# Centring the first half ahead of layer 1 and scaling by the reciprocal deviation after the expert pick

## The reference, cut to what matters

```python
def _layernorm(x, axis=-1, eps=1e-05):
    m = jnp.mean(x, axis=axis, keepdims=True)
    v = jnp.var(x, axis=axis, keepdims=True)
    return (x - m) / jnp.sqrt(v + eps)

# layer 1, E = 4 experts, W = ctx_2048, expert_ids from the token id
for e in range(E):
    g = jax.nn.silu(jnp.einsum('bsd,fd->bsf', hidden_states, Wg[e]))
    u = jnp.einsum('bsd,fd->bsf', hidden_states, Wu[e])
    y = jnp.einsum('bsf,df->bsd', g * u, Wd[e])
    out = jnp.where((expert_ids == e)[..., None], y, out)
x = x + layer_1(_layernorm(x))
x = x + layer_2(_layernorm(x))
```

## Time and profile before

| | us |
|---|---|
| median of 3 runs | 173.74 |
| lowest, highest of them | 173.63, 174.43 |
| the profiled execution, whole | 173.89 |
| its span in the trace | 171.8 |
| TensorE busy in the span | 166.6 (97%) |
| VectorE busy | 114.2 (66%) |
| ScalarE busy | 67.8 (39%) |
| GpSimd busy | 39.6 (23%) |

### The profile page before, as it was taken

The page is one execution under the profiler, slowest core; times in us unless marked ns, Lnnn a source line. Parts: engine busy times, 40 slices in busy tenths (PEclk is TensorE's granted clock), DMA queues, the critical chain, the costliest instruction groups (busy, mean ns, idle before and its releaser), DMA issues.

```text
span 171.8 us, 2194 instructions
## 1 busy us (share of the span) xinstructions
PE 166.6 (97%) x728; PEld 130.6 (76%) x728; DVE 114.2 (66%) x230; ACT 67.8 (39%) x112; POOL 39.6 (23%) x37
## 2 busy tenths in 40 slices
PE   6989999999999999999999999999999999999992
PEld 2568888888877888788787778788787887878881
DVE  0779778888984988588688528964744444444452
ACT  2472520551258254824664593152212222223320
POOL 2593000698200025539385000000000000000000
PEclk9999999999999999999999999999999999999999
DMA  4999000176400036742111200043361211100003
GB/s 137 307 373 352 23 4 2 25 236 227 122 0 4 15 130 181 203 160 67 61 61 61 61 0 4 8 126 126 113 195 45 75 65 61 62 0 4 2 0 122
DMA packets 7971, 16.41 MB, mean 95 GB/s; under 512 B 1336, under 2 KB 2200, under 8 KB 7832
## 3 DMA queue, kind: packets, MB, share of 16 engines
q1 hardware_dynamic: 7960, 16.27, 29.0%
HBM read 15.08 MB, written 1.18 MB: 95 GB/s over the span
## 4 chain that ended last, share of the span: by engine, by line
PE 97%; ACT 0%; POOL 0%; DVE 0%; issue 0%; DVEq 0%; POOLq 0%
PE bank L853 26%; PE bank L913 14%; PE bank L911 13%; PE bank L912 13%; PE bank L931 7%; PE bank L934 7%; PE bank L932 7%; PE bank L943 4%; PE bank L820 2%; PE bank L907 1%; PE bank L908 1%; PE bank L832 1%; ACT xn_hi L433 0%; POOL warm L383 0%; DVE xt L732 0%
## 5 line engine op out<-in xcount | busy, mean ns | idle before, releaser
L913 PE MATMUL bank<-xn_lo,gu_hi 128*128 128x512 f32 (+1 forms) x104 | 41.0, 394 | 0.0
L911 PE MATMUL bank<-xn_hi,gu_lo 128*128 128x512 f32 x96 | 37.9, 395 | 0.0
L912 PE MATMUL bank<-xn_hi,gu_hi 128*128 128x512 f32 x96 | 37.8, 394 | 0.0
L501 ACT ACTIVATE h_hi<-hid 128x512 fp32r<-128x512 f32 (+1 forms) x26 | 16.4, 632 | 45.7 <-DVE hid L720 45.7
L725 DVE TENSOR_TENSOR h_lo<-hid,h_hi 128x512 fp32r<-128x512 f32 (+1 forms) x26 | 20.2, 778 | 15.6 <-ACT h_hi L501 15.6
L913 PEld LDWEIGHTS bank<-xn_lo,gu_hi 128*128 128x128 f32 (+1 forms) x104 | 19.4, 186 | 5.0
L491 ACT ACTIVATE act_sb<-bank 128x512 f32<-128x512 f32 (+1 forms) x26 | 15.4, 594 | 18.1 <-PE bank L913 18.0
L398 POOL TENSOR_TENSOR gu_lo<-stage,gu_hi 128x512 fp32r<-128x512 f32 x12 | 17.9, 1516 | 17.6 <-ACT gu_hi L426 17.6
L912 PEld LDWEIGHTS bank<-xn_hi,gu_hi 128*128 128x128 f32 x96 | 18.0, 187 | 4.4
L911 PEld LDWEIGHTS bank<-xn_hi,gu_lo 128*128 128x128 f32 x96 | 18.0, 187 | 4.4
L931 PE MATMUL bank<-h_hi,wd_lo 128*128 128x512 f32 (+1 forms) x52 | 20.6, 396 | 0.0
(11 more groups left out here) (76 smaller groups left out, 213.1 us busy)
## 6 DMA issues: line engine op xcount, KB each, us to landing
stage<-gu_d SPq DMA_DIRECT2D x6, 512.0 KB, 3.5
stage<-wd_d SPq DMA_DIRECT2D x3, 512.0 KB, 4.1
x<-comb_d SPq DMA_DIRECT2D x8, 192.0 KB, 2.7
ids<-comb_d SPq DMA_DIRECT2D x8, 192.0 KB, 3.0
stage<-ctx_d SPq DMA_DIRECT2D x4, 256.0 KB, 5.0
xt<-xt_d SPq DMA_DIRECT2D x1, 1024.0 KB, 10.3
x<-comb_d SPq DMA_DIRECT2D x8, 128.0 KB, 3.1
ids<-comb_d SPq DMA_DIRECT2D x8, 128.0 KB, 2.8
```

Of the source, the lines that this page charges most:

```text
L911: nc.tensor.matmul(out[:], gu_lo[:, cols], xn_hi[:, h, k], start=(k == 0), stop=False)
L912: nc.tensor.matmul(out[:], gu_hi[:, cols], xn_hi[:, h, k], start=False, stop=False)
L913: ins = nc.tensor.matmul(out[0:rows, :], gu_hi[:, wide], xn_lo[:, h, k], start=False, stop=(k == KC - 1))
```

## The change

x of half 0 is only centred before layer 1: TensorE multiplies (x - mean), and the reciprocal deviation of each token multiplies the picked product z of mixes 0 and 1 (`scale`). As that product has tokens on columns, the deviations are needed as a row on all partitions: they are written to DRAM from their tile with four bytes per piece, and read back broadcast to 128 partitions. Half 1 and layer 2 are normalised as before. The mean of VectorE's tiles (0 and 2) comes from its statistics, that of ScalarE's tiles (1 and 3) from an accumulating pass (`minus_mean`). The identity comes in one load with the first two tiles. The first half of `xn_hi` is rounded by ScalarE for k = 0 and by VectorE for k = 1. Mix 0 has an order of its own (`first_mix`), in which the matmuls with the low weights of experts 1 to 3 come later. The warm-up has 8 matmuls, with 8 shorter ones placed between and behind the transposes. The diff, cut to its core:

```diff
-WARM_UP = 20
+WARM_UP = 8
...
             sp.dma_start(ids[:], ids_d.partition_broadcast(P)).then_inc(ids_in, 16)
+            sp.wait_ge(powered, 1)
+            sp.dma_start(rstd_d.rearrange("t c -> c t"), rstd[:, 0], allow_slow_non_contiguous=True).then_inc(rstd_out, 16)
+            sp.wait_ge(rstd_out, 16)
+            sp.dma_start(rstd_all[:], rstd_d.rearrange("t c -> (t c)").partition_broadcast(P)).then_inc(rstd_in, 16)
+            sp.wait_ge(rstd_in, 16)
             sp.dma_start(xt[:], xt_d).then_inc(xt_in, 16)
...
             nc.gpsimd.memset(comb[:], 0.0).then_inc(comb_zero, 1)
-            rstd_of(0, 1, slice(0, TT // 2))
-            rstd_of(0, 2, slice(TT // 2, TT))
-            for n in range(E1):
-                low_part(n)
-            rstd_of(1, 3)
+            low_part(0)
+            low_part(1)
+            rstd_of(0)
+            low_part(2)
+            low_part(3)
+            rstd_of(1)
...
+            def centre(t):
+
+                act.wait_ge(x_in[t // (TT // 2)], 16)
+                nc.scalar.activation(xn[:, t], x[:, t], ACT.Copy, scale=-1.0 / D,
+                                     accum_out=minus_mean[:, t:t + 1]).then_inc(astep, 1)
+                act.wait_ge(astep, t // 2 + 1)
+                nc.scalar.activation(xn[:, t], x[:, t], ACT.Identity, bias=minus_mean[:, t:t + 1]).then_inc(normed_a, 1)
...
             nc.scalar.preload_act_table(ACT.Silu)
-            apply_norm(0, range(TT // 2))
+            centre(1)
+            centre(3)
             high_part(0)
-            apply_norm(0, range(TT // 2, TT))
+            x_high("n1", 0, 0)
             high_part(1)
-            x_high("n1", 0, 0)
-            x_high("n1", 0, 1)
             high_part(2)
             high_part(3)
             first_z(0)
             apply_norm(1)
-            silu_z(0)
             first_z(1)
             x_high("n1", 1, 0)
             x_high("n1", 1, 1)
+            silu_z(0)
             silu_z(1)
...
+            def centre(t):
+
+                dve.wait_ge(x_in[t // (TT // 2)], 16)
+                tile_stats(0, t)
+                dve.wait_ge(dstep, steps[0])
+                step(nc.vector.bn_aggr(meanvar[:, 0, t], stats[:, t]))
+                dve.wait_ge(dstep, steps[0])
+                nc.vector.tensor_scalar(xn[:, t], x[:, t], meanvar[:, 0, t, 0:1], None, ALU.subtract).then_inc(normed_v, 1)
+
+            def scale(n):
+
+                dve.wait_ge(rstd_in, 16)
+                dve.wait_ge(z_picked, (n + 1) * (E1 - 1))
+                nc.vector.tensor_tensor(prod[:, n % 2], prod[:, n % 2], rstd_all[:], ALU.mult).then_inc(z_scaled, 1)
...
+            centre(0)
+            centre(2)
+            tile_stats(0, 1)
+            dve.wait_ge(side_done, side_at["n1", 0, 1] + 1)
+            nc.vector.tensor_scalar(xn_hi[:, 0, 1], side_bank("n1", 0, 1)[:], 1.0, None, ALU.mult).then_inc(xhi_done, 1)
             x_low("n1", 0, 0)
             x_low("n1", 0, 1)
+            tile_stats(0, 3)
+            layer_norm_vars(0, (1, 3))
...
             pick(0, masked[0], [1])
             layer_norm_apply(1)
             pick(0, masked[0], [2, 3])
-            hidden_1(0)
+            scale(0)
             x_low("n1", 1, 0)
             x_low("n1", 1, 1)
+            hidden_1(0)
             pick(1, masked[0])
+            scale(1)
             hidden_1(1)
...
+                pe.wait_ge(xhi_done, KC)
+                high(0)
+                weights_low(0, last=False)
+                high(1)
+                x_low(0, last=True)
+                x_low(1)
+                weights_low(1)
+                high(2)
+                x_low(2)
+                high(3)
+                x_low(3)
+                weights_low(2)
+                weights_low(3)
...
             pe.wait_ge(warm_set, 1)
-            for _ in range(WARM_UP):
-                nc.tensor.matmul(bank[7][:], warm[:, 0:P], warm[:], start=True, stop=True)
-            pe.wait_ge(consts_in, 16)
-            norm_transposes("n1", 0, 0)
-            mix(0)
+            keep_warm(WARM_UP)
+            pe.wait_ge(x_in[0], 16)
+            norm_transposes("n1", 0, 0, (0, 2, 2, 1))
+            keep_warm(3, HALF // 2)
+            first_mix()
```

More of the change, by code:

```diff
@@ L60 @@
 SPREADS = 4
+PAIR = TT // 2 * D
 RING = HALVES * KC
@@ L453, in silu_z @@
             def silu_z(n):
-                act.wait_ge(z_picked, (n + 1) * (E1 - 1))
+                if mixes[n][1] == 0:
+                    act.wait_ge(z_scaled, n + 1)
+                else:
+                    act.wait_ge(z_picked, (n + 1) * (E1 - 1))
                 if n >= 2:
@@ L812, in side_wait, with keep_warm, norm_transposes @@
                 return bank[b]
-            def norm_transposes(what, n, h):
+            def keep_warm(count, cols=HALF):
+                for _ in range(count):
+                    nc.tensor.matmul(bank[7][:, 0:cols], warm[:, 0:P], warm[:, 0:cols], start=True, stop=True)
+            def norm_transposes(what, n, h, between=()):
                 banks = [side_wait(what, h, k) for k in range(KC)]
                 for t in range(TT):
+                    if between:
+                        keep_warm(between[t], HALF // 2)
                     wait_normed(pe, n, t)
@@ L875, in mix, with first_mix, high, weights_low @@
                         between[e]()
+            def first_mix():
+                z = [ring_bank("z", 0, e)[:] for e in range(E1)]
+                f = slice(0, P)
+                def high(e):
+                    pe.wait_ge(w_hi, e + 1)
+                    for k in range(KC):
+                        nc.tensor.matmul(z[e], ctx_hi[:, e, k, f], xn_hi[:, 0, k], start=(k == 0), stop=False)
+                def weights_low(e, last=True):
+                    pe.wait_ge(w_lo, e + 1)
+                    for k in range(KC):
+                        ins = nc.tensor.matmul(z[e], ctx_lo[:, e, k, f], xn_hi[:, 0, k], start=False, stop=last and k == KC - 1)
+                    if last:
+                        ins.then_inc(z_done, 1)
+                def x_low(e, last=False):
+                    for k in range(KC):
+                        pe.wait_ge(xlo_done, k + 1)
+                        ins = nc.tensor.matmul(z[e], ctx_hi[:, e, k, f], xn_lo[:, 0, k], start=False, stop=last and k == KC - 1)
+                    if last:
+                        ins.then_inc(z_done, 1)
+                pe.wait_ge(xhi_done, KC)
[11 more added lines that the diff above has]
+                weights_low(3)
             def gate_or_up(g, up):
```

82 lines of the change are left out of this document (36 added, 46 removed).

## The result

The change is slower by far more than forecast: 186.84 us median (186.68 to 188.38, four runs) for 173.88 of the kernel before on the same chip (173.63 to 174.43, four runs), a ratio of 1.076, 95% interval 1.0697 to 1.0823. The prediction was 174.7 with a range up to 176.6. The direction was right, the size was not. The profiled execution has a span of 184.5 us for 171.8, so 12.7 us are to be found.

The account below looks back on a forecast made before the run. TensorE, busy 97% of the span, was taken as the bound, with VectorE having 1.28 us to spare. Opening -0.6 and stall +1.5 gave +0.95 on the profiled execution: 174.7 us predicted, range 173.3 to 176.6 (forecast's own 174.1 to 175.4).

Parts of the forecast that it names:

- The place and the chain of VectorE: First `x_low` of half 1 to `pick(4)` grows from 16.75 to 19.35 us; TensorE stalls 1.52 us for x1.
- The row by DMA: Deviations through DRAM: write 3.6 us, broadcast 2.9, row there at 18.5 (16.9 to 21.7), just in time for `scale(0)`.
- Rival A: The row comes late, each us past 18.7 a us of stall: total +2.2 to +4, about 176; chance 0.22.
- Size of the last add: Last add before x1's transposes takes 0.69 us if ahead of GpSimd's subtraction, up to 1.76 if behind: stall 1.1 to 2.2.
- Rival B: TensorE's clock is not up when mix 0 begins, transposes take 1 us more: about +1.7, 175.4; chance 0.10.
- The opening: Centring only, before layer 1: first matmul near 8.65, mix 1 at 15.0 instead of 15.58; gain 0.6 us, bounds 0 and 1.3.
- M: Time at which mix 1 can begin: 15.58 us in the kernel before, forecast 15.0.
- So no second stall follows: Behind the x1 stall both engines are delayed alike; VectorE waits 0.71 us for ScalarE before layer 2's critical `x_low`.

Follow-up runs that it names:

- row_at_once_full: Changed kernel without the row's two DMAs (half 0 deviations set to 1), shared down weights' low part on 128 partitions instead of 96: 175.69 us, ratio 1.0097.
- row_by_pe: Changed kernel with the row made by TensorE transposes and a ScalarE copy, shared down weights' low part on 128 partitions: 175.82 us, ratio 1.0116.
- price_writes: Kernel before plus six DMAs in a row behind its last output: 512 adjoining 4-byte pieces 8.23 us, spaced 256 B apart 2.13, 128 of 16 B 1.41.
- wd0_full: Changed kernel with the shared down weights' narrow piece cut on all 128 partitions instead of 96: 181.29 us, ratio 1.0432.
- fill_waits: Changed kernel with matmuls on zeros in TensorE's two long waits (20 and 22): 184.82 us.
- row_at_once_order: As row_at_once_full, with `hidden_1(0)` put back ahead of the two `x_low` of half 1: 175.73 us.
- opening: Kernel before with merged load, 14 warm-ups and fillers, split rounding and `first_mix`; half 0 normalised as before, no row or scaling: 179.94 us, ratio 1.0360.
- opening_full: As opening, with the shared down weights' low part cut on all 128 partitions: 174.53 us, ratio 1.0039.
- relief: row_by_pe with half 1's masks made by GpSimd and the first step of `pick(2)` moved into the wait for silu: 173.66 us, ratio 0.9997.
- gap: Changed kernel with GpSimd waiting, after its 96-partition subtraction, until VectorE has done `add_block_1(3)`: 180.08 us, ratio 1.0346.

## Why the prediction was wrong, point by point

**The place and the chain of VectorE: right.** The second stall stands where the prediction put it, released by `add_block_1`, and 19.35 us from `x_low` to `pick(4)` were measured as 19.34 (row_at_once_full) and 19.32 (row_by_pe). The stall came out as 1.70 to 1.73 in the trace's count, or 2.16 for 1.52 in the forecast's own (row_at_once_full), inside 1.1 to 2.2 either way.

**"The row by DMA": the first step that failed, by a mis-sized term.** The prediction had 3.6 for the write and 2.9 for the broadcast, bounds 5.8 and 3.9; they took 8.82 and 4.96. Its argument was that the time lies between "does not hang on pieces" and "hangs on pieces alone", both read from a store of 128 long pieces. Neither end covers it: spaced pieces, equal in number, took 2.13 us (price_writes). Pow ended at 10.74 and not at 12.0, so the row came at 24.55, after the latest bound of 21.7 even so. Rival A (the row is late) had the mechanism and a chance of 0.22. It put the whole loss at 2.2 to 4 us, 1.2 to 3.0 of them for the row; by wd0_full less row_at_once_full the row cost 5.6.
The Trainium skill, DMA: Bandwidth & Descriptors, section Anatomy of one DMA, lays most of the fixed cost of a DMA on the confirmation of the last byte. The trace agrees in kind, with seven us between the last packet and the end of the write; the page's about 2.0 us, given for another issue path, is near the spaced and the 16-byte writes (2.13 and 1.41), and far from the adjoining 4-byte one. Its section Specifications has small writes cost a read and a write of the target, below 512 B; the spaced pieces are as small and fast, so no rule by size alone fits these rows.

**"Size of the last add": the second step that failed.** The prediction took a lock's price as between none and one of GpSimd's instructions, 0.69 to 1.76. It applied that to the last addition alone and left `add_block_1(3)` at the 1.21 it had before, inside the 19.35. That 1.21 hung on a gap of 0.24 us in GpSimd's queue, which was in the trace of before. VectorE still meets GpSimd at the same point (0.09 for 0.10 us behind the narrow subtraction); it was ScalarE's rounding, now ahead of GpSimd's queue, that closed the gap. Its price by the rows: 6.16 for 1.21 is 4.95, the clock behind the longer wait adds 1.75, and the last addition, now behind GpSimd's series, took 0.69 for the 1.73 of wd0_full, which gives 1.04 back: 5.66, against 5.55 between the two medians.
The Trainium skill, SBUF - State Buffer, section Who interferes with whom, has the exclusion last for a whole instruction of the other engine; 1.20 and 1.73 us in wd0_full agree with it, 6.16 us over five instructions do not.

**The clock: named at the wrong place.** Rival B looked for a low clock at mix 0, where it stayed at 1.0. It fell in the two waits, with 1.75 us on the path. A forecast of a stall of over 4 us would have had to add it. The price that rival B named, slower transposes, did appear in other executions of the same opening (wd0_full, TensorE):

```profile
5.71 0.64 PE L860 MATMUL bank<-first,xn 128*128 128x128 f32 x2
```

Here a pair of transposes takes 0.43 us until the next group starts, in the change 0.22. The view's granted clock reads 1.00 in both; the spacing shows the low level. Where all groups ran at the full rate (the change, fill_waits, row_at_once_order), the first real matmul came at 7.44 to 7.56. Where two to six of them ran at half rate (the other seven profiles with 8 warm-ups), it came at 7.74 to 8.51. With 14 warm-ups (opening, opening_full) the transposes ran at the full rate.

**The opening: right in kind, too small.** Gain 1.71 in the profiled execution for 0.6, above the bound of 1.3. The pass with accumulation took 0.42 + 0.19 and the second 0.51, where 0.70 and 0.60 were taken; ScalarE's second tile was done at 5.97, not 7.2. Pow ended 1.3 us early, and the last four matmuls of mix 0, with the low weights, lost 0.38 us where 0.75 was forecast (1.31 us for four steps of 0.233). The gain differs between executions: with the same opening M was 14.91 in row_at_once_full. Part of that is the level at which the transposes ran, as above, and not the arrival of the tiles: in wd0_full the statistics began at 3.65 for 3.98, and the first real matmul came 0.84 later. Another part is the wait for the last low parts, 0.4 to 0.6 us in most of the profiles.

**"So no second stall follows": wrong by 0.41 us,** in row_at_once_full. The prediction looked for room at the `x_low` of layer 2; the stall came ahead of it, at the transposes. TensorE now turns x1 as soon as it is done, where before x1 lay ready for 0.66 us, so the cast (1.25) and the pick behind the addition are in the way: VectorE's statistics of x1 begin 1.66 us behind the start of the transposes for 1.07.

The forecast, with its steps at their measured size but with row and port in order: 0.95, -0.1 for an `x_low` at 19.30, +0.62 for the add (1.72 for 1.10), +0.41 for the second stall is 1.88; the spans are 173.7 and 171.8.

**What stays open.** Why a GpSimd instruction on 96 partitions lets the next ones shut VectorE out; why adjoining 4-byte writes are confirmed so late (price_writes shows what goes with it, not by which part of the memory path, nor whether spacing or order counts); which of the two changes of relief freed VectorE.

## What to carry to other kernels

When a change moves any engine against GpSimd's queue, list every VectorE instruction with two SBUF inputs that begins beside a series of GpSimd's, and ask which gap lets it in today and which third engine makes that gap: a kernel can owe 6 us to a gap of 0.24 that ScalarE's lateness makes. A handover through DRAM is priced by a store of the same piece size and spacing, not by one of the same bytes; turn the layout so that each partition writes one run, or turn it on TensorE. And an extra wait of some 5 us on TensorE costs more than itself, as the matmuls behind it ran at half rate for 3 to 5 us.

## What the runs showed of the hardware that was not expected

- 512 adjoining writes of 4 bytes: 8.2 to 8.8 us until confirmed, with packets moving in the first 1.4 us only. The same spaced by 256 B: 2.13. 128 of 16 B: 1.40 and 1.41. A broadcast of the 2 KB right behind the slow write: 4.74 and 4.96, behind the fast one 3.70 and 4.00.
- A VectorE addition with two SBUF inputs beside GpSimd's subtractions: 1.17 to 1.21 us in a series of 128-partition pieces, 6.12 to 6.16 in a series headed by a 96-partition piece without a gap, 1.19 to 1.21 with a gap of 0.24 or 0.63.
- ScalarE's pass of 256 columns with an accumulated sum is two records, 0.42 and 0.19 us.
- A comparison of 512 columns, int32 to uint8: 1.54 us on GpSimd, 0.36 on VectorE.
- The granted clock was 0.50 behind idle stretches of 3.9 (wd0_full, for 5 us of work), 4.9 and 5.5 us, and stayed 1.0 behind one of 1.7. Behind stretches of 3.7 (gap) and 4.0 us (opening) TensorE resumed at 1.00 and the clock fell to 0.50 about 1 us later, during work, for some 3 us.
